# A grouped circular convolution with group norm: own buffers for ScalarE's evictions, Newton steps one addition later, and loads issued behind a later store

## What is computed

```python
x: (32, 384, 56, 56) float32; weight: (384, 1, 56, 1); bias: (384,)

def _L0_conv_ref(x, weight, bias):
    x_cat = jnp.concatenate([x, x[:, :, :-1, :]], axis=2)      # rows repeat: the filter wraps around
    out = jax.lax.conv_general_dilated(x_cat, weight, window_strides=(1, 1), padding='VALID',
              dimension_numbers=('NCHW', 'OIHW', 'NCHW'), feature_group_count=x.shape[1])
    return out + bias[None, :, None, None]

def _gn(v, G=32, eps=1e-5):
    g = v.reshape(B_, G, C_ // G, H_, W_)
    m = jnp.mean(g, axis=(2, 3, 4), keepdims=True)
    s = jnp.var(g, axis=(2, 3, 4), keepdims=True)
    return ((g - m) / jnp.sqrt(s + eps)).reshape(v.shape)

x = x + _L0_conv_ref(_gn(x), L0_conv_weight, L0_conv_bias)
```

## Time and profile before

| what | value |
|---|---|
| median of 3 runs | 880.48 us (877.5 to 1353.82) |
| profiled execution, its own time | 881.76 us |
| its span, first to last instruction | 879.9 us |
| busy share of the span | PE 83%, DVE 77%, ACT 75%, POOL 65% |
| DMA queue q1: share of 16 engines | 99.1% |
| HBM read, written | 185.97 MB, 154.14 MB |
| mean granted TensorE clock | 0.925 |

### The profile page before, as it was taken

The page is one execution under the profiler, slowest core; times in us unless marked ns, Lnnn a source line. Parts: engine busy times, 40 slices in busy tenths (PEclk is TensorE's granted clock), DMA queues, the critical chain, the costliest instruction groups (busy, mean ns, idle before and its releaser), DMA issues.

```text
span 879.9 us, 8182 instructions
## 1 busy us (share of the span) xinstructions
PE 732.7 (83%) x1920; PEld 513.0 (58%) x1920; DVE 679.5 (77%) x1538; ACT 662.8 (75%) x1026; POOL 571.2 (65%) x1102
## 2 busy tenths in 40 slices
PE   0688898889889888878788887988878988889895
PEld 0456666666566666556565564665655656566664
DVE  7888878897787878778777677877877887788842
ACT  1788788788788878778677776787877867778784
POOL 2467767676676666666675656676766667567665
PEclk9999979998898999899898899899989989899998
DMA  9999999999999999999999999999999999999986
GB/s 355 410 387 399 383 407 396 406 413 410 403 394 374 377 391 389 405 392 388 401 381 396 370 361 386 398 403 398 403 389 387 392 402 400 390 401 409 405 306 229
DMA packets 39472, 340.64 MB, mean 387 GB/s; under 512 B 5008, under 2 KB 5120, under 8 KB 8704
## 3 DMA queue, kind: packets, MB, share of 16 engines
q1 hardware_dynamic: 39424, 340.13, 99.1%
HBM read 185.97 MB, written 154.14 MB: 387 GB/s over the span
## 4 chain that ended last, share of the span: by engine, by line
DMA 52%; PE 13%; POOL 13%; ACT 10%; DVE 8%; issue 3%; SPq 0%; POOLq 0%; ACTq 0%
DMA out<-xt 28%; DMA xt<-x 24%; PE conv L402 12%; POOL xt L235 10%; ACT xn L330 7%; DVE st L264 5%; ACT xn L338 3%; DVE xt L281 2%; PE p_mean L378 1%; POOL newt L227 1%; POOL rstd L228 1%; POOL newt L226 1%; POOL newt L225 1%; POOL shift L229 0%; PE p_var L387 0%
## 5 line engine op out<-in xcount | busy, mean ns | idle before, releaser
L402 PE MATMUL conv<-xn,runs 112*112 112x448 f32 x1536 | 694.5, 602 | 24.6 <-DMA runs<-taps 10.9
L330 ACT ACTIVATE xn<-xt,shift,rstd 112x672 f32<-112x672 f32 x512 | 463.1, 942 | 140.1 <-POOL xt L235 140.1
L402 PEld LDWEIGHTS conv<-xn,runs 112*112 112x112 f32 x1536 | 465.6, 314 | 167.3 <-issue 64.7
L264 DVE BATCH_NORM_STATS2 st<-xt 112x6 f32<-112x336 f32 x1024 | 451.4, 494 | 109.5 <-DMA xt<-x 109.3
L235 POOL TENSOR_TENSOR xt<-xt,xn 112x448 f32<-112x448 f32 x384 | 431.2, 1136 | 81.0 <-ACT xn L338 80.8
L281 DVE SCALAR_TENSOR_TENSOR xt<-conv,bias_all,xt 112x448 f32<-112x448 f32 x384 | 258.5, 673 | 81.1 <-PE conv L402 80.5
L338 ACT ACTIVATE xn<-conv,bias_all 112x448 f32<-112x448 f32 x384 | 235.7, 626 | 47.7 <-PE conv L402 44.9
L378 PE MATMUL p_mean<-msum,neg_mean 112*112 112x8 f32 x128 | 24.5, 263 | 112.2 <-POOL msum L204 112.2
L214 POOL TENSOR_TENSOR dev<-st,nmean 112x16 f32<-112x16 f32 x128 | 24.9, 216 | 134.6 <-ACT nmean L314 134.6
L378 PEld LDWEIGHTS p_mean<-msum,neg_mean 112*112 112x112 f32 x128 | 19.3, 191 | 150.2 <-POOL msum L204 134.4
L386 PEld LDWEIGHTS p_var<-st,avg 112*112 112x112 f32 x128 | 23.6, 210 | 40.6 <-POOL dev L218 25.9
(11 more groups left out here) (23 smaller groups left out, 69.4 us busy)
## 6 DMA issues: line engine op xcount, KB each, us to landing
xt<-x SPq DMA_DIRECT2D x128, 1344.0 KB, 10.6
out<-xt SPq DMA_DIRECT2D x128, 1176.0 KB, 12.9
runs<-taps SPq DMA_DIRECT2D x64, 147.0 KB
bias_all<-bias SPq DMA_DIRECT2D x1, 168.0 KB, 14.1
```

Source lines behind the costliest of these rows:

```text
L264: ins = nc.vector.bn_stats(st[:, n % RS, h, b, :], xt[0:P, n % XS, h, b * ROW:(b + 1) * ROW])
L330: ins = nc.scalar.activation(xn[:, n % NS, :, part], xt[0:P, n % XS, :, part], ACT.Identity, scale=rstd[:, n % RS, b:b + 1], bias=shift[:, ...
L402: nc.tensor.matmul(bank(c), lay[:, :, c], channel_of(xn, u % NS, c), start=True, stop=True).then_inc(conv_ready, 1)
```

## The change

Three things are changed.

1. ACT evicts into a new tile `kept` of KEEP = 4 buffers of one channel each, used in turn, and POOL adds from there. `normalize(n)` no longer waits for POOL's additions of unit n-2; instead each `evict` waits until POOL has made the addition that used the same buffer four evictions ago.
2. POOL makes `newton(u+2)` behind its fourth addition of unit u (channel 7), and no longer behind its third (channel 5).
3. SP's loop is written anew. Behind the store of (u, h) comes the load of (u+5, h), into the half-slot whose store was issued two halves before the newest one.

```diff
+KEEP = 4
+        kept = sb("kept", [P, KEEP, N])
+        def kept_of(u, c):
+            return kept[:, (through(ACT_CH, u, c) - 1) % KEEP, :].rearrange("k (b w) -> k b w", b=BP)
             for u in range(UNITS):
-                store(u, 0)
-                if u >= 1:
-                    load(u - 1 + XS, 1)
-                store(u, 1)
-                g = u // PER_GROUP + 2
-                if u % PER_GROUP == PER_GROUP - 1 and g < GROUPS:
-                    load_taps(g)
-                load(u + XS, 0)
+                for h in range(HALVES):
+                    store(u, h)
+                    g = u // PER_GROUP + 2
+                    if h == 1 and u % PER_GROUP == PER_GROUP - 1 and g < GROUPS:
+                        load_taps(g)
+
+                    if u >= 1:
+                        load(u - 1 + XS, h)
@@ gpsimd
-                nc.gpsimd.tensor_tensor(cell, cell, channel_of(xn, u % NS, c), ALU.add).then_inc(pool_added, 1)
+                nc.gpsimd.tensor_tensor(cell, cell, kept_of(u, c), ALU.add).then_inc(pool_added, 1)
-                for c in ACT_CH[:3]:
+                for c in ACT_CH[:4]:
                     add_x(u, c)
                 if n < UNITS:
                     newton(n)
-                for c in ACT_CH[3:]:
+                for c in ACT_CH[4:]:
                     add_x(u, c)
@@ scalar
                         act.wait_ge(conv_ready, (n - NS + 1) * CG)
-                        act.wait_ge(pool_added, through(ACT_CH, n - NS, CG))
             def evict(u, c):
-
                 act.wait_ge(conv_ready, u * CG + c + 1)
-                nc.scalar.activation(channel_of(xn, u % NS, c), bank_bw(c), ACT.Identity, bias=bias_of(u, c)
+                if through(ACT_CH, u, c) > KEEP:
+                    act.wait_ge(pool_added, through(ACT_CH, u, c) - KEEP)
+                nc.scalar.activation(kept_of(u, c), bank_bw(c), ACT.Identity, bias=bias_of(u, c)
                                      ).then_inc(act_evicted, 1)
```

## The result

The changed kernel takes 1,011.1 us in the median (1,003.35 to 1,018.84, 4 runs), the kernel before 881.64 us (4 runs, one more than above): the ratio is 1.149, 95% interval 1.142 to 1.156. I had predicted 885.7 us, within 2%. It is 15% slower, far outside the range of 867 to 900 us. All ratios compare undisturbed runs with undisturbed runs, so a ratio can differ a little from that of the medians beside it.

A forecast was written before the change was run, and what follows sets the result against it. The prediction took DMA bandwidth to bound the long middle at 13.55 us a unit. From 881.76 us profiled, +3.4 (head) +3.1 (end) -1.3 (tail) gave 887.0, less 1.3 to the median: 885.7 us, range 867 to 900.

The forecast's parts named there:

- What bounds the kernel before: Long middle: DMA bandwidth binds at 13.55 us a unit; SP's and ACT's waits lie behind a full DMA queue.
- The ring in the middle: ACT evicting into four buffers in turn: removes its 140.1 us of waits for POOL, worth 0 in the middle.
- The Newton steps and the cadence: POOL's Newton steps behind the fourth addition: compute cadence goes from 12.2 to about 12.1 us, under 13.55 us.
- The load order, head: Near 50 us: a load issued 3.4 us later leaves the DMA engines dry about as long, +3.4 us.
- The load order, middle: Middle: SP has more in flight, the queue stays full and the unit keeps 13.55 us, cost 0.
- End: Last load: one more store of 1.20 MB ahead of it, +3.1 us, bounds 0 and 3.5.
- Tail: Behind the last load: ACT's shorter waits for POOL give -1.3 us, bounds -4.1 and +1.1.
- B: Head, 50 to 240 us: DMA runs dry once a unit, 35 us over 14 units, 921 us; chance 0.04.
- A: Middle: DMA rate rises from 392 to 406 GB/s, 865.4 us, or to 430 GB/s, 834 us; chance 0.08.
- C: Middle: DMA rate falls to 370 GB/s as loads run beside stores of their own half, 921 us; chance 0.06.
- D: All units: ACT's wait was the bound, so the cadence falls from 13.55 to 12.1 us, 793 us; chance 0.02.

The follow-up runs named there:

- A kernel with the clock at 0.979: Two unread matrix multiplies on PE ahead of the mean, added to the kernel before: 883.12 us, ratio 0.997.
- the changed kernel with fillers: Three unread matrix multiplies on PE between channel 1 and the mean, added to the changed kernel: 874.66 us, ratio 0.994.

## Why the prediction was wrong

**What bounds the kernel before: right.** A kernel with the clock at 0.979 is as fast as one at 0.925, one without ACT's 140 us of waits too. The DMA bound of 13.55 us holds, and the waits that look largest in the profile (SP's 399 us, ACT's 140 us) are worth nothing.

**The ring in the middle, 0 us: right** (1.001, interval 0.992 to 1.010).

**The Newton steps and the cadence: this step failed.** I summed one round to 12.05 us and concluded "it stays under 13.55 us". Two things are wrong in it. First, the length at full clock: it is 12.80 us, which is still under 13.55 and would have done no harm. I had taken the 6.1 us from ACT's copy of the mean to the end of channel 7's eviction as ACT's own, from the earlier trace rows. But in those rows the copy came 1.8 us behind `mean`, so PE had a start on ACT. In the new chain the copy follows `mean` at once, and ACT waits for PE: 0.55 us ahead of channel 5. Second, and this is the loss of 130 us, I kept the clock fixed, although showed that it already stood at 0.92 and not at 1.00. The sum moved `msum` later in relation to PE's work and I had PE's wait in front of me, 1.60 us, but followed only what waits for the mean and not what PE itself does meanwhile. In the changed kernel PE stands idle for 1.8 to 2.6 us there; in the unit shown the granted clock goes from 1.00 to 0.50 behind it, and three channels take 4.83 us in place of 2.62. ACT's copy-to-eviction piece, 6.1 us in my sum, is 423.97 + 0.63 - 414.28 = 10.3 us in the unit shown above, with the row below. The round becomes 15.3 us in the mean, above the DMA bound, and 64 units of some 2 us more are the loss.

```profile
423.97 0.63 ACT L343 ACTIVATE kept<-conv,bias_all 112x448 f32<-112x448 f32 x1 [0.24 <-PE conv L407]
```

The rows also show how it spreads: at the lower clock PE holds up ACT, ACT holds up POOL's fourth addition and the Newton steps, and the two sums wait behind these. That this also makes PE's next wait longer, and so keeps the clock low, fits the rows, but no run isolates it.

The Trainium skill, "TensorE: Matmul & The Clock Gate", section HAM oscillation, describes this pattern: waits that come back ahead of every tile can throw the clock back every time, and the work should be ordered so that PE stays busy. In kind this case's runs agree: 0.801 with the wait, 0.994 with the same wait filled. In size they do not: the section speaks of longer waits than the 1.8 to 2.7 us that come back here in the middle, and by its rule these would have done no harm. The measurement decides.

**The load order, head: the gap is there.** In the kernel with the load order alone the stretch from 46 to 60 us has a DMA share of 0.82, so 0.18 x 14 = 2.5 us are lost; my term was 3.4. The first load into a used half-slot is issued at 53.30 us there, as predicted (52.97). In the changed kernel itself the same stretch has a share of 0.71, which is 4.1 us. The stretches of the kernel with the load order alone, and that row of its SP queue:

```profile
46.00:60.00 14.00, 12.35 (x35) 8.98 (x36) 11.21 (x26) 11.97 (x19) 8.94 (x18) 0.97 0.82 293
240.00:830.00 590.00, 507.30 (x1306) 349.44 (x1306) 460.66 (x1046) 450.29 (x697) 385.19 (x738) 0.90 1.00 394
```

```profile
53.30 0.42 SPq L138 DMA_DIRECT2D xt<-x  x1
```

**The load order, middle: right in kind.** In that kernel landings take 17.0 and 14.6 us, about the 15 to 17 that I had expected, and the long stretch moves 394 GB/s against 392:

```profile
xt<-x SPq DMA_DIRECT2D x128, 1344.0 KB, 17.0
out<-xt SPq DMA_DIRECT2D x128, 1176.0 KB, 14.6
```

**End: right in kind. Tail: not tested by itself.** In the kernel with the load order alone the last load is issued at 822.46 us, and the last four loads take 15.6 to 17.2 us to land, so it lands between 838.1 and 839.7 us. Before it was 834.1, and I had said near 840. The term of -1.3 us for the tail is smaller than what the runs can tell. With the load order alone the median came out at 893.3 us, above the 887 that my terms for head and end give; what makes up the rest is open.

```profile
822.46 0.74 SPq L138 DMA_DIRECT2D xt<-x  x1
```

```profile
DMA to landing us min/median/max: 15.6/15.9/17.2
```

**The rivals.** B was the nearest: "it decides where the compute cadence lies over 13.55 us". That condition came true, with 15.3 us. Its mechanism did not: I had put it in the head, gave it 0.04 and priced it by gaps in the queue, 921 us. My argument against it was the 12.1 us of the failed step, so the one wrong sum carried both the forecast and the dismissal of the rival. A fall of PE's clock was not among the rivals at all. A and C did not occur: wherever the DMA was the bound, the long stretch ran at 390 to 401 GB/s with the new order and at 392 to 403 with the old one. D is refuted by the ring alone, 1.001. (The 2 us that B quotes from the Trainium skill, "DMA: Bandwidth & Descriptors", are given there for DMAs that GpSimd issues; those of this kernel are SP's, so the agreement in size proves little.)

## What to carry to other kernels

A step that is moved has to be followed to PE too, even when PE has time to spare: ask how long PE will now stand idle and what clock it gets behind that, and price its work at both levels. Where a cadence is under the bound by a tenth, a halved PE clock is a rival with a price of its own. If a wait of PE can't be avoided, give PE work to do in it, or put the waiting matmul behind work that is ready; here one channel took back most of the loss.

## What the runs showed of the hardware

Waits for the sums of 2.3 us a unit in the mean went with a mean clock of 0.80 (the changed kernel), of 1.9 us with 0.89 (mean behind channel 2), of 1.6 us with 0.925 (before); the first wait of an execution, 14.1 us, is left out in each. The length of one wait alone does not tell the level. In the kernel before, a wait of 2.39 us has the three channels behind it at full speed, 2.62 us, and one of 1.53 us has them at 3.69:

```profile
407.81 0.36 PE L378 MATMUL p_mean<-msum,neg_mean 112*112 112x8 f32 x2 [2.39 <-POOL msum L204]
408.03 2.62 PE L402 MATMUL conv<-xn,runs 112*112 112x448 f32 x6
```

```profile
275.78 0.36 PE L378 MATMUL p_mean<-msum,neg_mean 112*112 112x8 f32 x2 [1.53 <-POOL msum L204]
276.00 3.69 PE L402 MATMUL conv<-xn,runs 112*112 112x448 f32 x6
```

In the changed kernel with fillers PE waits for `take` 12 times, for up to 3.0 us, and the clock is 0.994. What decides between the levels stays open.

```profile
PE conv L407 <- DVE xt L286: 14.5, 12, 3.0
```
